# Query projection of a second attention layer by seven block products in place of eight

## The chip, the cores and the metric

The kernel runs on one core of a Trainium2 chip. The metric is the device time of one execution in microseconds. Engines are named as in the profile: PE is TensorE's matmuls and PEld its weight loads, DVE is VectorE, ACT ScalarE, POOL GpSimd, SP the engine that issues most DMAs.

## The reference, cut to what matters

Two gated layers act on x of 16 x 64 tokens by 512, each a cross-attention with 32 query heads and 8 key and value heads of 128 and then a small network. The change is in the attention of the second layer:

```python
q = (hidden_states @ Wq.T).reshape(bsz, q_len, H, HD).transpose(0, 2, 1, 3)
q = _rmsnorm(q, q_norm_w)
k = _rmsnorm(k, k_norm_w)
scores = einsum('bhqd,bhkd->bhqk', q, k) * scale + mask
out = einsum('bhqk,bhkd->bhqd', softmax(scores), v)
return out.reshape(...) @ Wo.T
```

Everything is float32. The kernel splits both operands of each large product into a high and a low part (hi + lo) and sums three matmuls, hi by hi, hi by lo and lo by hi.

## The kernel before

**Tiling.** The 1024 tokens are held transposed, hT_hi and hT_lo of [128, 4, 1024]: four k-tiles of the 512 features on the partitions, tokens along the row. Heads go in 8 groups (g) of J = 4 heads that share a key head, and tokens in two halves (h) of 512. A step (g, h) is one group and one half, unit u = 2g + h. The steps are software-pipelined over three units: step (g, h) projects the queries of unit u, does scores and softmax of unit u - 1 and finishes unit u - 2 with values and the output product. `att_steps` (L881) writes out groups 0, 1 and 7 and loops over 2 to 6.

**TensorE** (`att_pe`, L924 to L1060) does in each steady step of the second layer, in this order: scores of u - 1 (L978), sums of squares for the norm (L953), values of u - 2 (L1005), four heads of projection (`project`, 12 matmuls of 512 columns each through `three`, L226 to L228, into the two banks ps_q) and four token tiles of output product (`project_out`, 12 matmuls each). A head's projection waits for ScalarE's reading (q_rot) of the bank two heads before.

**ScalarE** (`att_act`) computes Ln and Exp of the norm's sums (L1160, L1162), then per head a square (q_sq, L1150) and a copy scaled by the product of the two norm weights (qT, L1153), the high parts of values' results (o_hi, L1191), the softmax exponential (p_sb, L1177), the high part of the probabilities (p_hi, L1184), and the high parts of the next group's weights: wo_hi (L1142) in h = 0, wq_hi (L737) in h = 1.

**VectorE** (`att_dve`, step L1532) does in one step: two transposes of the sums of squares to r_t and eight small copies to r_s (L1457), the transpose of the scores to s_sb (L1435), the scaling by the norm (L1479), the mask (L791), maxima (mx_a L1490, four mx_c L1485), o_lo twice (L1518), two folds of q_sq (L1470), o_lo twice, the sums (sm_a L1502, four sm_c L1485, p_rec), two additions to x_sb (L1529), the transpose of the probabilities (pT, L1512), two folds, p_lo (L808), two additions.

**GpSimd** (`att_pool`, step L1319) does in h = 0 four wo_lo (L1310; the second waits for VectorE's r_s), in h = 1 four wq_lo (L743) between the rest, and in every step the shift of the scores by the maxima (L797) and the normalisation of the probabilities (L803).

**Order and queues.** Each engine works through its list strictly; the order is written by hand in the four `step` functions. SP loads wo, the spilled keys and values and the next wq (`att_wq_split`, L746, waits until both parts of the group before are split). PSUM is full: two banks ps_q, two of ps_s for scores, four ps_b.

## Time and profile before

| | us |
|---|---|
| median of 3 runs | 1179.61 (1178.96 to 1181.38) |
| profiled execution, its own time | 1179.01 |
| span of the profiled execution | 1177.1 |
| a step of the second layer, start of scores to start of scores | 26.08 |

The profile page is one execution. Busy time of PE comes from modelled ends, since matmuls overlap: their pitch is read from the start times in the order of time. TensorE's granted clock is at full speed (2.4 GHz) in all forty slices. In the second layer the scores of step (1,1) start at 787.9, of (2,0) at 813.9, of (2,1) at 840.0, of (3,0) at 866.1, and each next step 26.07 later up to (7,0) at 1074.7.

### The profile page before, as it was taken

Reading aid. Unit: us, or ns where it says so; the run is one execution under the profiler, and the core shown is the slowest. Engines: PE = TensorE matmul, PEld = TensorE weight load, DVE = VectorE, ACT = ScalarE, POOL = GpSimd, SP = SyncE. Lnnn points to the kernel's source line nnn. Section 1 sums busy time; section 2 is a strip of 40 time slices with the busy share of each in tenths; the row PEclk is TensorE's granted clock in tenths of the full one; section 3 lists DMA queues with packets and bytes.
Section 4 is the critical chain, followed back from the end, with each engine's and each line's share of the span. In section 5 each row is a group of like instructions: output and inputs, shape, how many; then the busy total and the mean of one; then the engine's idle time right before and its main releaser. Section 6 shows DMA issues by size and latency. Waiting matters only on the chain.

```text
span 1177.1 us, 17132 instructions
## 1 busy us (share of the span) xinstructions
PE 1169.5 (99%) x6272; PEld 946.7 (80%) x6272; DVE 880.9 (75%) x1538; ACT 424.0 (36%) x748; POOL 532.9 (45%) x371
## 2 busy tenths in 40 slices
PE   9999999999999999999999999999999999999998
PEld 8888888888788888777788888777777777777776
DVE  4656646898888888889984335798888887888695
ACT  5145152322322222231552123535453443435542
POOL 5522533766667676677463112305242433425410
PEclk9999999999999999999999999999999999999999
DMA  7944735812211221211210003121221221121101
GB/s 286 285 137 159 211 111 162 287 55 81 81 66 59 89 80 45 80 45 45 99 64 36 1 1 107 55 94 57 91 80 45 80 80 54 71 89 39 43 1 72
DMA packets 57315, 106.54 MB, mean 91 GB/s; under 512 B 3633, under 2 KB 36529, under 8 KB 51889
## 3 DMA queue, kind: packets, MB, share of 16 engines
q1 hardware_dynamic: 56736, 104.82, 26.0%
q0 software_dynamic: 384, 1.05, 0.2%
q8 instruction: 32, 0.52, 0.2%
q14 instruction: 19, 0.15, 0.0%
q10 hardware_dynamic: 144, 0.00, 0.0%
HBM read 78.59 MB, written 27.26 MB: 90 GB/s over the span
## 4 chain that ended last, share of the span: by engine, by line
PE 96%; DVE 2%; issue 0%; ACT 0%; DVEq 0%; POOL 0%; POOLq 0%
PE ps_q L226 14%; PE ps_b L226 14%; PE ps_b L228 14%; PE ps_b L227 14%; PE ps_q L227 13%; PE ps_q L228 13%; PE ps_s L978 5%; PE ps_b L1005 4%; PE ps_s L278 1%; PE ps_q L953 1%; PE ps_q L2152 1%; PE ps_b L479 1%; PE ps_s L1847 1%; PE ps_q L529 0%; PE ps_b L529 0%
## 5 line engine op out<-in xcount | busy, mean ns | idle before, releaser
L226 PE MATMUL ps_q<-hT_hi,wq_hi 128*128 128x512 f32 x512 | 203.2, 397 | 0.0
L227 PE MATMUL ps_q<-hT_lo,wq_hi 128*128 128x512 f32 x512 | 199.6, 390 | 0.0
L228 PE MATMUL ps_q<-hT_hi,wq_lo 128*128 128x512 f32 x512 | 199.2, 389 | 0.0
L226 PE MATMUL ps_b<-wo_hi,o_hi 128*128 128x512 f32 x440 | 171.6, 390 | 0.0
L227 PE MATMUL ps_b<-wo_lo,o_hi 128*128 128x512 f32 x440 | 171.2, 389 | 0.0
L228 PE MATMUL ps_b<-wo_hi,o_lo 128*128 128x512 f32 x440 | 171.2, 389 | 0.0
L743 POOL TENSOR_TENSOR wq_lo<-wq_raw,wq_hi 128x512 fp32r<-128x512 f32 x64 | 90.2, 1413 | 112.8 <-ACT wq_hi L737 112.8
L1317 POOL TENSOR_TENSOR qT<-q_t 128x512 f32<-128x512 f32 x64 | 89.8, 1405 | 66.3 <-DVE q_t L1430 60.8
L226 PEld LDWEIGHTS ps_q<-hT_hi,wq_hi 128*128 128x128 f32 x512 | 96.1, 188 | 24.3 <-issue 1.5
L228 PEld LDWEIGHTS ps_q<-hT_hi,wq_lo 128*128 128x128 f32 x512 | 96.1, 188 | 20.3
L227 PEld LDWEIGHTS ps_q<-hT_lo,wq_hi 128*128 128x128 f32 x512 | 96.2, 188 | 18.7
L1310 POOL TENSOR_TENSOR wo_lo<-wo_raw,wo_hi 128x512 fp32r<-128x512 f32 x56 | 83.5, 1507 | 56.4 <-ACT wo_hi L1142 38.3
L1184 ACT ACTIVATE p_hi<-pT 128x1024 fp32r<-128x1024 f32 x32 | 34.0, 1061 | 189.7 <-DVE pT L1512 189.7
L226 PEld LDWEIGHTS ps_b<-wo_hi,o_hi 128*128 128x128 f32 x440 | 82.6, 188 | 18.4 <-issue 1.4
L228 PEld LDWEIGHTS ps_b<-wo_hi,o_lo 128*128 128x128 f32 x440 | 82.6, 188 | 17.1
L227 PEld LDWEIGHTS ps_b<-wo_lo,o_hi 128*128 128x128 f32 x440 | 82.6, 188 | 17.1
L1529 DVE SCALAR_TENSOR_TENSOR x_sb<-ps_b,gates,x_sb 128x512 f32<-128x512 f32 x115 | 81.4, 722 | 18.0 <-PE ps_b L228 17.5
L803 POOL TENSOR_TENSOR p_sb<-p_sb,p_rec 128x1024 f32<-128x1024 f32 x29 | 55.7, 1920 | 83.8 <-DVE p_rec L1506 83.8
L1518 DVE TENSOR_TENSOR o_lo<-ps_b,o_hi 128x512 fp32r<-128x512 f32 x128 | 81.8, 682 | 12.6 <-ACT o_hi L1191 10.7
L1191 ACT ACTIVATE o_hi<-ps_b 128x512 fp32r<-128x512 f32 x128 | 66.5, 607 | 34.0 <-PE ps_b L1005 26.7
L1177 ACT ACTIVATE p_sb<-s_sb,zero_b 128x1024 f32<-128x1024 f32 x32 | 37.2, 1162 | 96.9 <-POOL s_sb L797 93.5
L797 POOL TENSOR_TENSOR s_sb<-s_sb,mx_c 128x1024 f32<-128x1024 f32 x28 | 53.8, 1921 | 32.1 <-DVE mx_c L1485 32.1
(301 smaller groups left out, 2498.0 us busy)
## 6 DMA issues: line engine op xcount, KB each, us to landing
wq_raw<-in_wq SPq DMA_DIRECT2D x16, 1024.0 KB, 4.8
wo_raw<-in_wo SPq DMA_DIRECT2D x16, 1024.0 KB, 4.8
kT<-kT_spill SPq DMA_DIRECT2D x32, 256.0 KB, 4.3
v_hi<-v_hi_spill SPq DMA_DIRECT2D x16, 512.0 KB, 3.7
v_lo<-v_lo_spill SPq DMA_DIRECT2D x16, 512.0 KB, 4.7
v_hi_spill<-vs_hi SPq DMA_DIRECT2D x12, 512.0 KB, 5.4
v_lo_spill<-vs_lo SPq DMA_DIRECT2D x12, 512.0 KB, 6.7
kw_raw<-in_wk SPq DMA_DIRECT2D x4, 1024.0 KB, 9.2
```

Source lines behind the costliest of these rows:

```text
L226: nc.tensor.matmul(dst, l_hi, r_hi, start=first, stop=False)
L227: nc.tensor.matmul(dst, l_hi, r_lo, start=False, stop=False)
L228: return nc.tensor.matmul(dst, l_lo, r_hi, start=False, stop=last)
L743: nc.gpsimd.tensor_tensor(wq_lo[:, :, j * D:(j + 1) * D], wq_raw[:, :, j * D:(j + 1) * D], wq_hi[:, :, j * D:(j + 1) * D].bitcast(F32), AL ...
L797: eng.tensor_tensor(sc, sc, wide(mx_c[:, :], QB), ALU.subtract).then_inc(c["s_shifted"], 1)
L803: eng.tensor_tensor(pr, pr, wide(p_rec[:, :], QB), ALU.mult).then_inc(c["p_normed"], 1)
L978: last = nc.tensor.matmul(ps_s[par * S:(par + 1) * S, t * JS:(t + 1) * JS], kT[:, h, b:b + S], qT[:, h, :, b:b + S], start=True, stop=True)
L1191: nc.scalar.activation(o_hi[:, 2 * half:2 * half + 2, :, par * S:(par + 1) * S], ps_b[n].rearrange("p (t j q) -> p t j q", t=2, j=J), ACT. ...
L1310: nc.gpsimd.tensor_tensor(lo, wo_raw[:, j, :], hi.bitcast(F32), ALU.subtract).then_inc(c["wo_lo"], 1)
L1317: nc.gpsimd.tensor_tensor(qT[:, h, j, :], q_t1[:, j % 2, :], q_t2[:, j % 2, :], ALU.add).then_inc(c["q_rot"], 1)
L1518: nc.vector.tensor_tensor(o_lo[part], ps_b[n].rearrange("p (t j q) -> p t j q", t=2, j=J), o_hi[part].bitcast(F32), ALU.subtract).then_inc ...
L1529: nc.vector.scalar_tensor_tensor(x_sb[:, i, :], out_bank(u, t)[:, :], gates[:, lay:lay + 1], x_sb[:, i, :], ALU.mult, ALU.add).then_inc(c[ ...
```

## The change

For groups W0 = 3 to 6 of the second layer (`woven`), the product of the 512 x 512 weights of a group and the 512 x 512 tokens of a half is cut into 2 x 2 blocks of 256 and computed by seven block products and sums of blocks:

- of the weights (blocks a11, a12, a22 and one below s1's place): s1, s2, s3, s4, four sums of [128, 2, 256] on GpSimd in float32 (`woven_sums` in h = 0 of the group before, `woven_last_sum` in h = 1), and seven high parts on ScalarE and seven low parts on GpSimd in place of four of each; all 512 elements a partition;
- of the tokens: t1 to t4, [128, 2, 512] each for both halves, once, on GpSimd in steps (1,0) to (2,1), 10 operations of 1024 elements; four high parts on ScalarE, four low parts on GpSimd;
- each product is 12 matmuls of 256 columns (two head columns, two k-tiles, three parts), 84 in a step where there were 48 of 512;
- of the results: two products accumulate in one bank (a11 with a12, s3 with a22, s1 with s4); ScalarE copies the first product to qT, and VectorE makes five joins of a PSUM bank with a part of qT (512 elements each). The first head pair's first block is copied by ScalarE alone.

In these steps ScalarE also makes the eight r_s copies (the function `last_sums`, L1164, that was used once, renamed), VectorE folds the squares in two operations of [64, 4, 256] in place of four of [64, 2, 256], the transposed probabilities are written to s_sb and not to pT (so the scores' transpose waits for p_lo), and VectorE adds one output tile before and three after the turn of the probabilities in place of two and two. Steps (2,0), (2,1), (6,0) and (6,1) are written out, not in the loop. The norm weights are multiplied into the keys in the first phase (ScalarE, `kv_stage_keys`) and their DMA and product move there; the query copies lose their scale. Some semaphore increments that nobody waits for go, and buffers move. One launch argument, the scratch size for dynamic DMAs, becomes 2048.

The diff, cut to its core:

```diff
+        WOVEN_PARTS = ("a11", "s2", "s3", "a12", "s1", "a22", "s4")
+        def woven_sums(pool, gt):
...
+            nc.gpsimd.tensor_tensor(s1_f, s1_f, a22, ALU.add).then_inc(c["s_f"], 1)
+            nc.gpsimd.tensor_tensor(s2_f[:, :, :], s1_f, a11, ALU.subtract).then_inc(c["s_f"], 1)
+            nc.gpsimd.tensor_tensor(s3_f[:, :, :], a22, s2_f[:, :, :], ALU.subtract).then_inc(c["s_f"], 1)
+            def project_woven(g, h):
...
+                def product(bank, name, right, first, last_one=False):
+                    if h == 0:
+                        pe.wait_ge(*c("woven_hi", turn)); pe.wait_ge(*c("woven_lo", turn))
+                    for q in range(2):
+                        for k in range(2):
...
+                pe.wait_ge(*c("ssq_t", u))
+                if h == 0:
+                    pe.wait_ge(*c("t_hi", 4))
+                    pe.wait_ge(*c("t_lo", 4))
+                product(ps_q[0], "a11", tokens(0, 0), True).then_inc(c["product"], 1)
+                product(ps_q[1], "s2", mixed(t2_hi, t2_lo), True, True).then_inc(c["product"], 1)
+                pe.wait_ge(*c("s_turned", u))
+                product(ps_h[0], "s3", mixed(t3_hi, t3_lo), True).then_inc(c["product"], 1)
+                pe.wait_ge(*c("copied", n + 1))
+                product(ps_q[0], "a12", tokens(1, 0), False, True).then_inc(c["q_done"], 1)
+                product(ps_h[1], "s1", mixed(t1_hi, t1_lo), True).then_inc(c["q_done"], 1)
+                pe.wait_ge(*c("joined", 5 * n + 2))
+                product(ps_h[0], "a22", mixed(t4_hi, t4_lo), False, True).then_inc(c["q_done"], 1)
+                pe.wait_ge(*c("joined", 5 * n + 3))
+                product(ps_h[1], "s4", tokens(1, 1), False, True).then_inc(c["q_done"], 1)
@@ ScalarE
+            def woven_step(g, h, next_wq):
+                sums_by_quadrant(us)
+                norms(us)
+                nc.scalar.activation(qT[:, h, 0:2, late], heads(ps_q[0]), ACT.Copy).then_inc(c["copied"], 1)
+                for n in range(4): out_high(up, n)
+                nc.scalar.activation(q_sq[:, 0:2, early], heads(ps_q[0]), ACT.Square).then_inc(c["q_sq"], 1)
+                nc.scalar.activation(qT[:, h, 0:2, early], heads(ps_q[0]), ACT.Copy).then_inc(c["q_rot"], J)
+                exponentials(us)
...
+                probs_high(us)
@@ GpSimd
+            def woven_step(g, h, next_wq):
+                if h == 0:
+                    for name in WOVEN_PARTS[4:]:
+                        woven_low(pool, g, name)
+                    for j in range(J):
+                        wo_low(g - 1, j)
+                elif building:
+                    woven_low(pool, g + 1, "a11")
+                att_shift(pool, lay, u - 1)
+                if h and building:
+                    woven_last_sum(pool, g + 1)
+                att_normalise(pool, lay, u - 1)
+                if h == 0 and not (isinstance(g, int) and g == G - 2):
+                    woven_sums(pool, g + 1)
+                elif building:
+                    for name in WOVEN_PARTS[1:4]:
+                        woven_low(pool, g + 1, name)
+                if second_opening(lay, g, h):
+                    att_normalise(pool, lay, us)
+                    pool.wait_ge(*c("p_lo", us + 1))
+                    mixed_first(t1_f, t1_t, (0, 1), (0, 0))
+                    mixed_joined(t1_f, t1_t, 3)
+                if (g, h) == (1, 1):
+                    att_wq_low(pool, lay, 2, 0)
+                    att_shift(pool, lay, us)
+                    pool.wait_ge(*c("p_exp", us + 1))
+                    mixed_first(t3_f, t3_t, (1, 1), (0, 1))
+                    att_normalise(pool, lay, us)
+                    for j in range(1, J):
+                        att_wq_low(pool, lay, 2, j)
+                    pool.wait_ge(*c("p_lo", us + 1))
+                    mixed_joined(t3_f, t3_t, 6)
+                    mixed_next(t2_f, (1, 1), t1_f, 8, 3)
+                if (g, h) == (2, 0):
+                    for j in range(J):
+                        wo_low(1, j)
+                    att_shift(pool, lay, us)
+                    pool.wait_ge(*c("p_exp", us + 1))
+                    mixed_next(t4_f, (1, 0), t2_f, 10, 8)
+                    att_normalise(pool, lay, us)
+                    woven_sums(pool, W0)
+                    pool.wait_ge(*c("p_lo", us + 1))
+                    mixed_low(t1_lo, t1_hi, t1_f, 1)
+                if builds_woven(lay, g, next_wq):
+                    mixed_low(t3_lo, t3_hi, t3_f, 2)
+                    woven_last_sum(pool, W0)
+                    att_shift(pool, lay, us)
+                    pool.wait_ge(*c("p_exp", us + 1))
+                    mixed_low(t2_lo, t2_hi, t2_f, 3)
+                    woven_low(pool, W0, "a11")
+                    att_normalise(pool, lay, us)
+                    for name in WOVEN_PARTS[1:4]:
+                        woven_low(pool, W0, name)
+                    mixed_low(t4_lo, t4_hi, t4_f, 4)
@@ VectorE
+            def woven_step(g, h):
+                turn_sums(us, 1 - h, True)
+                turn_scores(us, 1 - h)
+                scale_scores(us)
+                joined(part_b, ps_q[1], part_b)
+                att_mask(dve, lay, us, 1 - h)
+                joined(part_d, ps_h[0], part_b)
+                maxima(us)
+                joined(part_d, ps_h[1], part_d)
+                out_low(up, 0)
+                out_low(up, 1)
+                joined(qT[:, h, 2:4, early], ps_h[0], part_b)
+                out_low(up, 2)
+                joined(part_b, ps_h[1], part_b)
+                out_low(up, 3)
+                sums(us)
+                add_output(up, h, 0)
+                fold_woven(u, 0)
+                turn_probs(us)
+                fold_woven(u, 1)
+                att_probs_low(dve, lay, us)
+                for t in range(1, PAIRS):
+                    add_output(up, h, t)
```

## Rows read from the trace of the kernel before

**Rows 1.** Page: engines' busy us, share, instructions; the ending chain by engine

```profile
PE 1169.5 (99%) x6272; PEld 946.7 (80%) x6272; DVE 880.9 (75%) x1538; ACT 424.0 (36%) x748; POOL 532.9 (45%) x371
...
PE 96%; DVE 2%; issue 0%; ACT 0%; DVEq 0%; POOL 0%; POOLq 0%
```

**Rows 2.** Order of time, TensorE: start us, us, line, tiles; one step, the next's start

```profile
918.23 1.95 PE L978 MATMUL ps_s<-qT,kT 128*64 128x256 f32 x16
...
920.70 0.39 PE L1005 MATMUL ps_b<-p_hi,v_hi 64*128 64x256 f32 x2
920.93 0.28 PE L1005 MATMUL ps_b<-p_lo,v_hi 64*128 64x256 f32 x2
...
922.12 0.28 PE L1005 MATMUL ps_b<-p_hi,v_lo 64*128 64x256 f32 x2
922.32 0.50 PE L226 MATMUL ps_q<-hT_hi,wq_hi 128*128 128x512 f32 x1
...
944.31 1.95 PE L978 MATMUL ps_s<-qT,kT 128*64 128x256 f32 x16
```

**Rows 3.** Order of time, TensorE, opening of the layer; and one group of the whole span

```profile
741.20 0.39 PE L228 MATMUL ps_q<-hT_hi,wq_lo 128*128 128x512 f32 x1
741.43 0.60 PE L278 MATMUL ps_s<-ident,ln_buf 128*128 128x128 f32 x4
...
L278 PE MATMUL ps_s<-ident,ln_buf 128*128 128x128 f32 x92 | 12.4, 273 | 0.4 <-DVE ln_buf L266 0.2 <-DVE hT_lo L288 0.2
```

**Rows 4.** Order of time, VectorE: the last addition of that step

```profile
944.42 0.75 DVE L1529 SCALAR_TENSOR_TENSOR x_sb<-ps_b,gates,x_sb 128x512 f32<-128x512 f32 x1 [0.18 <-PE ps_b L228]
```

**Rows 5.** Order of time of the same step: GpSimd, then VectorE

```profile
923.38 5.83 POOL L1310 TENSOR_TENSOR wo_lo<-wo_raw,wo_hi 128x512 fp32r<-128x512 f32 x3 [3.05 <-DVE r_s L1457]
...
923.25 1.25 DVE L1435 STREAM_TRANSPOSE s_sb<-ps_s 128x1024 f32<-128x1024 f32 x1
924.61 1.23 DVE L1479 TENSOR_TENSOR s_sb<-s_sb,r_q 128x1024 f32<-128x1024 f32 x1
925.87 2.20 DVE L791 TENSOR_TENSOR s_sb<-s_sb,mask_sb 128x1024 f32<-128x1024 f32 x1
928.10 1.22 DVE L1490 TENSOR_REDUCE mx_a<-s_sb 128x32 f32<-128x1024 f32 x1
```

**Rows 6.** Groups, 866 to 1075: xcount, busy us, mean ns; last: one line's min/median/max ns

```profile
L1529 DVE SCALAR_TENSOR_TENSOR x_sb<-ps_b,gates,x_sb 128x512 f32<-128x512 f32 x34 | 24.7, 726 | 11.0 <-PE ps_b L228 11.0
...
L1518 DVE TENSOR_TENSOR o_lo<-ps_b,o_hi 128x512 fp32r<-128x512 f32 x32 | 20.6, 686 | 6.1 <-ACT o_hi L1191 4.9
...
L743 POOL TENSOR_TENSOR wq_lo<-wq_raw,wq_hi 128x512 fp32r<-128x512 f32 x16 | 20.8, 1298 | 64.8 <-ACT wq_hi L737 64.8
...
L797 POOL TENSOR_TENSOR s_sb<-s_sb,mx_c 128x1024 f32<-128x1024 f32 x8 | 15.4, 1921 | 6.8 <-DVE mx_c L1485 6.8
...
L1457 DVE COPY r_s<-r_t 32x16 f32<-32x16 f32 x64 | 10.7, 167 | 1.4
...
L1485 DVE TENSOR_TENSOR mx_c<-mx_a 32x32 f32<-32x32 f32 x32 | 5.9, 186 | 0.6
...
L791 DVE TENSOR_TENSOR s_sb<-s_sb,mask_sb x15: 1217/1226/2203, 752.4 to 1126.1; 128x1024 f32<-128x1024 f32 x15
```

**Rows 7.** GpSimd's durations of L808; order of time: VectorE in (1,0), TensorE in (3,0)

```profile
L808 POOL TENSOR_TENSOR p_lo<-pT,p_hi x13: 2382/2397/3464, 243.2 to 550.6; 128x1024 fp32r<-128x1024 f32 x13
...
786.92 0.69 DVE L1470 TENSOR_TENSOR q_sq<-q_sq 64x512 f32<-64x512 f32 x1
787.64 1.23 DVE L808 TENSOR_TENSOR p_lo<-pT,p_hi 128x1024 fp32r<-128x1024 f32 x1
...
870.18 0.50 PE L226 MATMUL ps_q<-hT_hi,wq_hi 128*128 128x512 f32 x1
```

**Rows 8.** ScalarE's durations (min/median/max ns) of two lines

```profile
L1171 ACT ACTIVATE r_s<-r_t x8: 226/228/230, 1121.2 to 1122.9; 32x16 f32<-32x16 f32 x8
...
L1160 ACT ACTIVATE r_q<-r_s,eps_rms x16: 321/322/323, 749.7 to 1123.1; 128x32 f32<-128x32 f32 x16
```

More of the change, by code:

```diff
@@ L945, in project @@
                 last.then_inc(c["q_done"], 1)
+            def project_woven(g, h):
+                u = 2 * g + h
+                n = u - 2 * W0
+                left = {name: woven_parts(name)[1:] for name in WOVEN_PARTS}
+                tok = [slice(h * HALF + a * QT, h * HALF + (a + 1) * QT) for a in range(2)]
+                own = slice(h * QT, (h + 1) * QT)
+                tokens = lambda rows, a: (hT_hi[:, 2 * rows:2 * rows + 2, tok[a]], hT_lo[:, 2 * rows:2 * rows + 2, tok[a]])
+                mixed = lambda hi, lo: (hi[:, :, own], lo[:, :, own])
+                def product(bank, name, right, first, last_one=False):
+                    if h == 0:
+                        turn = 7 * (g - W0) + WOVEN_PARTS.index(name) + 1
+                        pe.wait_ge(*c("woven_hi", turn))
+                        pe.wait_ge(*c("woven_lo", turn))
+                    l_hi, l_lo = left[name]
+                    r_hi, r_lo = right
+                    for q in range(2):
+                        for k in range(2):
+                            col = slice(q * D, (q + 1) * D)
+                            dst, closes = bank[:, q * QT:(q + 1) * QT], last_one and (q, k) == (1, 1)
+                            nc.tensor.matmul(dst, l_hi[:, k, col], r_hi[:, k, :], start=first and (q, k) == (0, 0), stop=False, skip_group_check=True)
+                            nc.tensor.matmul(dst, l_hi[:, k, col], r_lo[:, k, :], start=False, stop=False, skip_group_check=True)
+                            last = nc.tensor.matmul(dst, l_lo[:, k, col], r_hi[:, k, :], start=False, stop=closes, skip_group_check=True)
+                    return last
+                pe.wait_ge(*c("ssq_t", u))
[13 more added lines that the diff above has]
+                product(ps_h[1], "s4", tokens(1, 1), False, True).then_inc(c["q_done"], 1)
@@ L1067, in step @@
                         values(up, h, g - 1)
+                if woven(lay, g):
+                    project_woven(g, h)
+                    for t in range(PAIRS):
+                        project_out(up, h, g - 1, t)
+                    return
                 at_first = lay and isinstance(g, int) and (g, h) == (0, 0)
@@ L1152, in queries @@
                     ln_high(act, lns[2], NT - 1)
[L1153 removed]
+                nc.scalar.activation(qT[:, h, j, :], bank[:, :], ACT.Copy).then_inc(c["q_rot"], 1)
             def norms(u):
@@ L1434, in turn_scores @@
                 dve.wait_ge(*c("scored", u + 1))
+                if lay and not (isinstance(u, int) and (u < 4 or u == 2 * G - 1)):
+                    dve.wait_ge(*c("p_lo", u))
                 nc.vector.transpose(s_sb[:, :], ps_s[:, :]).then_inc(c["s_turned"], 1)
@@ L1471, in fold_squares, with fold_woven @@
                     dve.wait_ge(*c("q_fold", 4 * u + 2 * pair + r + 1))
+            def fold_woven(u, r):
+                own, tok = fold_part(r)
+                other = fold_part(1 - r)[0]
+                dve.wait_ge(*c("q_sq", 4 * u + 2 * r + 2))
+                nc.vector.tensor_tensor(q_sq[own, :, tok], q_sq[own, :, tok], q_sq[other, :, tok], ALU.add).then_inc(c["q_fold"], 2)
             def scale_scores(u):
@@ L1534, in step @@
                 if before_closing(lay, g, h):
+                    return
+                if woven(lay, g):
+                    woven_step(g, h)
                     return
```

278 lines of the change are left out of this document (239 added, 39 removed).

## The prediction

> **What bounds the kernel now.** I read the page's engine line and chain line first. TensorE shows work in 1169.5 of 1177.1 us, VectorE in 880.9, GpSimd in 532.9, ScalarE in 424.0. The chain of waits that ends last is TensorE for 96% and VectorE for 2% [rows 1]. So the end is set by the number of matmuls and their pitch, and by any moment at which TensorE must wait. The profiled execution took 1179.01 us (span 1177.1 and 1.9 around it), 0.6 under the median 1179.61 of the runs; I sum against the execution and give the result against the median.
>
> TensorE's own order of time shows one step of the second layer [rows 2]: scores at 918.23, values at 920.70, query projection at 922.32, and the next step's scores at 944.31. A step is 26.08 us, and no row in it shows a wait. I write times as distance from the step's start: values at 2.47, the projection at 4.09. A 512-column matmul comes every 0.227 us (0.23 by the rounded starts [rows 3]), so 48 of the projection take 10.9 and 48 of the output product another 10.9.
>
> VectorE has 1.6 us of slack at the end of a step: its last x_sb addition ends at 945.17, and the values that need its bank come at 944.31 + 2.47 = 946.78 [rows 2, 4]. Beside it, the two orders of time of VectorE and GpSimd for the same microseconds matter most [rows 5]. The mask addition takes 2.20 us where a run without GpSimd beside it takes 1.22, and three wo_lo subtractions take 5.83 together where three of their size, as wq_lo at 1.30, would take 3.9 [rows 5, 6]. The score scaling at 924.61 was not slowed, the mask after it was: a GpSimd operation that stood queued ran between the two, then the mask, then the next. So a VectorE operation with both inputs in SBUF and a GpSimd operation run one after the other. Reductions, transposes and operations that read PSUM (o_lo 0.69, x_sb 0.73 [rows 6]) run undisturbed beside GpSimd: mx_a at 928.10 takes its usual 1.22.
>
> The Trainium skill, SBUF — State Buffer, says the same where it lists which operations take the port that the two engines share: an exclusive lock for the whole instruction, taken by a VectorE instruction with two SBUF inputs against a GpSimd one that reads SBUF. By that rule all of GpSimd's new subtractions contend, and the trace agrees (2.20 against 1.22).
>
> **The change, part by part.** *TensorE.* In eight steps (groups 3 to 6, two each) 48 matmuls of 512 columns become 7 x 12 = 84 of 256 columns, each with its own full weight load. No row has this shape. Pairs of 256-column matmuls on half the rows come every 0.119 us (ten pitches from 920.93 to 922.12) [rows 2], and 128-column matmuls with a full weight load each every 0.11 (four in 0.60, of which the record of one is 0.27) [rows 3], so the load can keep up with 0.11. I take 0.120, the nearest row in columns: 84 x 0.120 = 10.1, minus 10.9, is -0.8 a step, -6.4 in all. The bounds are 0.11 (-1.6 a step, -13) and 0.130, where the gain is nil.
>
> The Trainium skill, TensorE: Matmul & The Clock Gate, section on packing small matmuls, says that a weight load overlaps matmuls in flight only when its row group differs. By that, load and stream add up for each of the 84. The sum does not use it: at 0.227 for 512 columns in the same row groups the trace disagrees.
>
> *VectorE, steady.* Added per step are five joins (PSUM plus qT, 512 elements): 5 x 0.69 = 3.5 (as o_lo [rows 6]). Eight r_s copies of 0.167 go to ScalarE (-1.4), four folds of 0.69 [rows 7] become two of 1.22, my estimate from the mask's 1024 elements (-0.3). Net +1.8 in a step with 1.6 of slack. The copies on ScalarE take 8 x 0.24 = 1.9 and Ln and Exp 0.32 each [rows 8]. r_t is ready when today's copies begin, 1.4 before the transpose at 5.02 [rows 5], so r_q comes at 3.6 + 1.9 + 0.7 = 6.2, no later than today's scaling at 6.38. ScalarE, 36% busy, has room for the rest: its qT copies lose a scale, it squares and copies as much as before.
>
> *The place where it bites.* The last product needs the third join, which the diff puts behind scale, join, mask, join and the maxima. Products start at 4.1 + n x 1.44: the seventh could start at 12.7. VectorE, second half of a group: scale 6.4 to 7.6, join 8.3, mask 9.5, join 10.2, mx_a 11.4, four mx_c of 0.186 12.2, join 12.9: 0.2 late. First half of a group: GpSimd now has seven queued subtractions there (three woven weights, four wo_lo) in place of four, so the mask waits 1.0 as today: 13.9, 1.2 late. That is 1.4 for two steps. If a mx_c also meets a subtraction it is one more microsecond, if none does nothing; both kept.
>
> *End of a step.* The first fold stands before the turn of the probabilities and has two SBUF inputs, so it waits for GpSimd's normalisation (1.92), then takes 1.22, where today the turn follows at once. p_lo and three additions then end near 28 to 30, against values at 26.1 + 2.5 = 28.6 [rows 2]. I take 0.35 a step. So the steady stretch is 4 x 1.4 + 8 x 0.35 = +8.4 against -6.4: +2.0.
>
> *GpSimd before group 3.* Ten operations on 128x1024 build the four token mixes, four more take their low parts. With two full SBUF inputs 1024 elements take 2.40 [rows 7], so 14 x 2.4 = 33.6 us, none of which exists today. All must be done between p_lo of step (1,0), which ends at 788.87, and the projection of (3,0) at 870.18 [rows 7]: 81.3 us. In the same window GpSimd has four wq_lo and four wo_lo (8 x 1.3), six shifts and normalisations (6 x 1.92 [rows 6]) and eight woven sums and splits (8 x 1.3): 32.3. Total 65.9. VectorE's operations that exclude GpSimd count per step (eight r_s 1.34, scale 1.23, mask 1.22, mx_c and sm_c 8 x 0.186, folds 4 x 0.69, p_lo 1.23), 9.3 in all and 27.8 in three steps [rows 5 to 7]. The two together need 93.7 in 81.3. A queued subtraction holds the port for less than its record: wo_lo, mask and wo_lo follow each other from 925.84 to 929.21, which leaves 1.08 for each wo_lo [rows 5]. Since not all will queue I take 0.12 off each of 36, 4.3. So the window must grow by 8.1 even with no gap. I take 8.1. Late r_s and mx_c are what TensorE will feel: r_q comes late, ScalarE's query copies stand behind it in its queue, and the third head's projection waits for them; in (2,0) the output product waits for wo_lo, queued behind 7.2 us of mixes. The bounds: 0 if the port yields more than I read, and 18 with the gaps: GpSimd waits for the exponential (1.2) in three steps and both engines for each other's softmax part, about 2 a step.
>
> *The rest.* The norm weights' product and their DMA move into the first phase: the DMA is issued before x's, for which VectorE waits in the same place, and the scale goes from ScalarE's query copies to its key copies, an engine in use 36% of the time. Nothing. The DMA of the query weights waits for all seven splits; these end in the next step, its data is needed a step later. Nothing, unless GpSimd runs over a whole step.
>
> **Sum.** -6.4 + 8.4 + 8.1 = +10.1, or 1179.0 + 10.1 = 1189.1 for the profiled execution and **1189.7** for the median.
>
> **Rivals.** *The port does not decide (faster).* If GpSimd's operations fall into VectorE's reductions, transposes and PSUM reads, only the products' 6.4 remains: 1173.2. For it: these free stretches make up over half of VectorE's step, and two waits in the diff (for p_exp, for p_lo) keep mixes out of part of the exclusive work. Against it: 93.6 in 81.3, and the mask is delayed today with four subtractions queued. It decides where fewer than one exclusive operation per step is held up.
>
> *The port decides more (slower).* Every one of eight small copies or four mx_c can meet another queued 2.4 us mix; the bound 18 in place of 8.1, so 1199.6.
>
> *The products are not cheaper.* At a pitch of 0.14 the 84 take 11.8, +0.9 a step; the joins then wait less, and +7 replaces about +2: 1194.7. Serial loading is a rival of its own: 0.120 + 0.109 = 0.229 each, 19.2 for 10.9, +66: about 1255. The 512-column pitch speaks against it; it is the skill's packing rule named above.
>
> *A draw.* If the transition costs 4 in place of 8.1 and no product waits in first halves, the sum is near 0: 1179.6.
>
> **How the numbers follow.** My forecast has 0.44 (its own range 1184 to 1196), the faster rival 0.24, the draw 0.10, the worse port 0.16, the dear products 0.05, serial loading 0.01. About 0.2% is what a measurement of this kernel can tell from no change. Faster is 0.24, same 0.10, slower 0.44 + 0.16 + 0.05 + 0.01 = 0.66. The range for 8 in 10 is 1173 to 1203: below it the cheap pitches of the faster rival, above it the worst of the port and serial loading.
>
> **What would show it.** Right: the 256-column rows at 0.12 pitch; steps of groups 3 to 6 near 26.3 on average, with TensorE idle before the seventh product released by VectorE's qT; mask, r_s, mx_c and folds with means far above their clean ones; the start of group 3's scores at 874, not 866. Wrong: steps of 25.3, or scores of group 3 at 866, or r_s copies at 0.167 all through.

## The result, and the profile after

The changed kernel takes 1202.08 us (median of 6, 1201.29 to 1203.65), the kernel before, run beside it, 1179.45 (6 runs, 1178.96 to 1181.38). The ratio is 1.0191, 95% interval 1.0178 to 1.0204: 22.6 us slower, where 10.1 had been forecast; it lies 0.9 below the upper end of the range. The profiled execution took 1201.29, with a span of 1199.5 against 1177.1, so 22.4 us have to be found.

Below, the *mixes* are GpSimd's fourteen operations for t1 to t4 (ten for the blocks, four low parts), a *pair* is the steps (g,1) and (g+1,0), and an instruction is *held* when it lasts longer than the same instruction does with the other engine idle.

The page of the changed kernel, engines and the ending chain by engine, answers to [rows 1]:

```profile
PE 1170.2 (98%) x6560; PEld 956.9 (80%) x6560; DVE 931.7 (78%) x1498; ACT 438.0 (37%) x812; POOL 624.4 (52%) x413
...
PE 73%; DVE 20%; issue 6%; ACT 1%; POOL 1%; DMA 0%; DVEq 0%; SPq 0%; ACTq 0%
```

TensorE has as many busy us as before in a longer span. VectorE's share of the chain went from 2% to 20%, and 6% is "issue". GpSimd got 91.5 us more, VectorE 50.8, though VectorE has 40 instructions fewer.

Where the time went is read from the starts of the scores of each step. The stretches between them, in the windows view of the changed kernel (columns: stretch, length, busy us and instructions of PE, PEld, DVE, ACT, POOL, granted TensorE clock, DMA share, GB/s):

```profile
787.60:819.60 32.00, 26.83 (x154) 20.77 (x155) 30.28 (x39) 13.80 (x25) 21.40 (x11) 1.00 0.12 42
819.60:854.00 34.40, 30.45 (x154) 23.34 (x154) 31.12 (x39) 10.69 (x18) 24.48 (x14) 0.85 0.20 69
854.00:883.80 29.80, 26.56 (x153) 20.52 (x152) 28.24 (x39) 15.60 (x28) 19.32 (x12) 1.00 0.13 45
883.80:911.60 27.80, 26.85 (x188) 22.05 (x188) 25.70 (x33) 10.00 (x22) 22.21 (x13) 0.94 0.24 86
911.60:937.20 25.60, 25.21 (x189) 21.61 (x188) 23.51 (x34) 13.53 (x29) 14.32 (x8) 1.00 0.15 52
937.20:964.60 27.40, 25.52 (x191) 21.70 (x190) 25.46 (x34) 12.19 (x26) 21.08 (x13) 1.00 0.25 86
...
1095.40:1124.10 28.70, 27.14 (x163) 20.86 (x162) 23.65 (x38) 13.21 (x24) 17.73 (x11) 1.00 0.13 47
```

The scores of (1,1) start at 787.57, in the kernel before at 787.71 (not at 787.9, as stated above for it): what moved into the first phase costs nothing. Steps (1,1), (2,0) and (2,1) took 96.3 us; the kernel before has 78.4 there (26.23, 26.07, 26.07). That is 17.9 of the 22.4. I call these three steps the opening. Step (3,0), the first of the new kind, is 1.7 longer than before; the seven after it lose 1.2 together (a pair is 52.9 against 52.14); (7,0), a plain step behind them, takes 28.7 in place of 27.1, 1.6 more.

The opening, in the order of time of the changed kernel (start us, us, engine, line, operation), GpSimd's and VectorE's rows of one stretch together, then TensorE's:

```profile
788.81 2.38 POOL L1558 TENSOR_TENSOR t_f<-hT_hi 128x1024 f32<-128x1024 f32 x1 [4.06 <-DVE p_lo L918]
791.15 2.39 POOL L1559 TENSOR_TENSOR t_t<-hT_lo 128x1024 f32<-128x1024 f32 x1
793.62 2.40 POOL L1563 TENSOR_TENSOR t_f<-t_f,t_t 128x1024 f32<-128x1024 f32 x1
...
791.04 5.74 DVE L1785 COPY r_s<-r_t 32x16 f32<-32x16 f32 x8
...
809.43 2.93 DVE L1820 TENSOR_TENSOR sm_c<-sm_a 32x32 f32<-32x32 f32 x4
...
816.06 3.41 DVE L1798 TENSOR_TENSOR q_sq<-q_sq 64x512 f32<-64x512 f32 x2
...
824.66 8.47 DVE L1785 COPY r_s<-r_t 32x16 f32<-32x16 f32 x8
...
819.56 3.51 PE L1136 MATMUL ps_s<-qT,kT 128*64 128x256 f32 x16 [3.24 <-issue]
...
830.62 0.39 PE L255 MATMUL ps_q<-hT_hi,wq_lo 128*128 128x512 f32 x1
834.96 0.76 PE L253 MATMUL ps_q<-hT_hi,wq_hi 128*128 128x512 f32 x1 [3.95 <-ACT qT L1316]
835.52 0.63 PE L254 MATMUL ps_q<-hT_lo,wq_hi 128*128 128x512 f32 x1
...
883.83 2.94 PE L1136 MATMUL ps_s<-qT,kT 128*64 128x256 f32 x16 [2.32 <-DVE q_sq L1798]
```

Eight copies of 0.167 us each [rows 6] take 5.74 in (1,1) and 8.47 in (2,0): a copy ends only when the GpSimd operation beside it ends, GpSimd then starts the next one, and a copy behind waits again. Eleven of the 24 copies of the opening were held, for up to 2.3 us; four of those in (2,0) by a wo_lo of 1.3 and not by a mix. The query norm's factors come late by that much, ScalarE's query copies stand behind them, and TensorE waits 3.95 for the bank.

The waits of 3.24 and 2.32 are of another kind: scores need the folded squares, and the folds stand beside low parts on GpSimd; before the 3.24, beside wq_lo, they take 3.41 for two of 0.69 (they end at 819.47, the scores start at 819.56).

Behind the 3.95 twelve matmuls come every 0.425 and not every 0.227; the sixteen scores behind the 3.24 take 3.51 and not 1.95. The granted clock of 834.9 to 840.2 is 0.50 and of 819.5 to 823.1 it is 0.54, that is the lower of TensorE's two levels, 1.2 GHz. The two cost 2.4 + 1.6 = 4.0 us on top of the waits. Behind the 2.32 the clock of 884.4 to 887.8 is 0.53: 3.4 us at the lower level, by my estimate 1.7 lost, in (3,0).

GpSimd itself is not the limit of the opening: the windows above have it busy 21.4 + 24.5 + 19.3 = 65.2 us of 96.2, idle for 31. Nor do the shift and the normalisation stand behind mixes: from (1,1) to (7,0) each of them starts 0.08 us after VectorE's instruction that releases it.

Groups of the changed kernel, 780 to 1100 us (xcount, busy us, mean ns, idle before and its releaser), which answer to [rows 6]:

```profile
L1806 DVE TENSOR_TENSOR q_sq<-q_sq 64x1024 f32<-64x1024 f32 x16 | 34.0, 2122 | 0.5
...
L918 DVE TENSOR_TENSOR p_lo<-s_sb,p_hi 128x1024 fp32r<-128x1024 f32 x10 | 22.1, 2206 | 0.3
L1875 DVE TENSOR_TENSOR qT<-ps_s,qT 128x512 f32<-128x512 f32 x32 | 21.8, 682 | 0.3
...
L1785 DVE COPY r_s<-r_t 32x16 f32<-32x16 f32 x24 | 18.9, 786 | 0.4
...
L1163 PE MATMUL ps_b<-p_hi,v_hi 64*128 64x256 f32 x92 | 14.6, 305 | 8.5 <-DVE x_sb L1864 8.4
```

The 24 copies of the three opening steps took 18.9 where they would be 4.0. The joins cost what was said (0.682, read from PSUM, undisturbed), but the new folds take 2.12 and not 1.22. TensorE's idle time in the woven steps (groups 3 to 6) stands before the values and is ended by VectorE's last x_sb; before the seventh product it is 1.6 in all. The end of (4,1) and the values of (5,0) behind it, in the order of time, with a row of the end of (4,0) last, answer to [rows 2, 4, 5]:

```profile
997.37 0.28 PE L1085 MATMUL ps_q<-t_lo,s_hi 128*128 128x256 f32 x1
997.49 0.28 PE L1086 MATMUL ps_q<-t_hi,s_lo 128*128 128x256 f32 x1
...
994.09 0.39 PE L1163 MATMUL ps_b<-p_hi,v_hi 64*128 64x256 f32 x2 [1.41 <-DVE x_sb L1864]
...
983.32 1.92 POOL L913 TENSOR_TENSOR p_sb<-p_sb,p_rec 128x1024 f32<-128x1024 f32 x1 [2.62 <-DVE p_rec L1841]
985.20 3.55 POOL L825 TENSOR_TENSOR s_lo<-s_f,s_hi 128x512 fp32r<-128x512 f32 x2
...
983.85 2.48 DVE L1806 TENSOR_TENSOR q_sq<-q_sq 64x1024 f32<-64x1024 f32 x1
...
987.51 2.32 DVE L1806 TENSOR_TENSOR q_sq<-q_sq 64x1024 f32<-64x1024 f32 x1
989.86 2.20 DVE L918 TENSOR_TENSOR p_lo<-s_sb,p_hi 128x1024 fp32r<-128x1024 f32 x1
...
963.24 2.20 DVE L918 TENSOR_TENSOR p_lo<-s_sb,p_hi 128x1024 fp32r<-128x1024 f32 x1
```

The new products come every 0.12. At the end of (4,1) the first fold stands behind the normalisation (2.48 for 1.22), the second fold (2.32) and p_lo (2.20) behind low parts of the next weights, and the values of (5,0) come 1.41 late. At the end of (4,0) only the first fold and p_lo (the row at 963.24, behind a sum of weights) are held, and the values of (4,1) come 0.38 late.

### The profile page after: what moved, and what is told of

It reads as the page before. It is cut to its first block, busy times and chain, and to the rows that moved or that the text cites. A ratio compares the mean times of both kernels' runs of the same rounds, so it can differ in the third digit from the quotient of the medians.

```text
span 1199.5 us, 17752 instructions
## 1 busy us (share of the span) xinstructions
PE 1170.2 (98%) x6560; PEld 956.9 (80%) x6560; DVE 931.7 (78%) x1498; ACT 438.0 (37%) x812; POOL 624.4 (52%) x413
## 4 chain that ended last, share of the span: by engine, by line
PE 73%; DVE 20%; issue 6%; ACT 1%; POOL 1%; DMA 0%; DVEq 0%; SPq 0%; ACTq 0%
PE ps_b L253 10%; PE ps_b L255 10%; PE ps_b L254 10%; PE ps_q L253 10%; PE ps_q L255 9%; PE ps_q L254 9%; PE ps_s L1136 3%; PE ps_b L1163 3%; DVE o_lo L1853 2%; DVE x_sb L1864 2%; DVE qT L1875 2%; DVE q_sq L1806 2%; DVE r_s L1785 2%; DVE mx_a L1825 1%; DVE sm_a L1837 1%
## 5 line engine op out<-in xcount | busy, mean ns | idle before, releaser
L253 PE MATMUL ps_q<-hT_hi,wq_hi 128*128 128x512 f32 x384 | 154.0, 401 | 4.9 <-ACT qT L1316 4.9
L254 PE MATMUL ps_q<-hT_lo,wq_hi 128*128 128x512 f32 x384 | 150.7, 392 | 0.0
L255 PE MATMUL ps_q<-hT_hi,wq_lo 128*128 128x512 f32 x384 | 150.4, 392 | 0.0
L253 PEld LDWEIGHTS ps_b<-wo_hi,o_hi 128*128 128x128 f32 x440 | 82.6, 188 | 19.5 <-issue 2.8
L253 PEld LDWEIGHTS ps_q<-hT_hi,wq_hi 128*128 128x128 f32 x384 | 72.7, 189 | 25.0 <-issue 5.9
L255 PEld LDWEIGHTS ps_q<-hT_hi,wq_lo 128*128 128x128 f32 x384 | 72.6, 189 | 15.6
L254 PEld LDWEIGHTS ps_q<-hT_lo,wq_hi 128*128 128x128 f32 x384 | 72.7, 189 | 14.1
L849 POOL TENSOR_TENSOR wq_lo<-wq_raw,wq_hi 128x512 fp32r<-128x512 f32 x48 | 71.8, 1506 | 23.0 <-ACT wq_hi L769 23.0
L1354 ACT ACTIVATE o_hi<-ps_b 128x512 fp32r<-128x512 f32 x128 | 66.9, 608 | 34.9 <-PE ps_b L1163 27.6
L675 POOL TENSOR_TENSOR kw_lo<-kw_raw,kw_hi 128x512 fp32r<-128x512 f32 x28 | 36.2, 1297 | 68.9 <-ACT kw_hi L631 68.9
```

Source lines behind the costliest of these rows:

```text
L253: nc.tensor.matmul(dst, l_hi, r_hi, start=first, stop=False)
L254: nc.tensor.matmul(dst, l_hi, r_lo, start=False, stop=False)
L255: return nc.tensor.matmul(dst, l_lo, r_hi, start=False, stop=last)
L849: nc.gpsimd.tensor_tensor(wq_lo[:, :, j * D:(j + 1) * D], wq_raw[:, :, j * D:(j + 1) * D], wq_hi[:, :, j * D:(j + 1) * D].bitcast(F32), AL ...
L1354: nc.scalar.activation(o_hi[:, 2 * half:2 * half + 2, :, par * S:(par + 1) * S], ps_b[n].rearrange("p (t j q) -> p t j q", t=2, j=J), ACT. ...
```

## The experiments

My theory after the result: each instruction of VectorE that excludes GpSimd waits for one whole queued operation, small or large, and what costs is how many of them meet one (the port). Its rivals: GpSimd's queue is simply longer, so that its shift, normalisation and wo_lo come late (the queue); and VectorE is full with five more joins (the joins). All differences are against the kernel before, run on the same chip.

**e1, without the token mixes.**

```diff
-                nc.gpsimd.tensor_tensor(by_half(f), quarters(hT_hi, *l), quarters(hT_hi, *r), ALU.subtract).then_inc(c["t_f"], 1)
+                return
...
-                mixed = lambda hi, lo: (hi[:, :, own], lo[:, :, own])
+                mixed = lambda hi, lo: tokens(0, 1)
```

> The changed kernel without the four token mixes: their ten operations, four high and four low parts are left out, and the products that use them read plain tokens. If GpSimd's token mixes are what the transition costs (17.7 of the 22.6 us at the start of group 3's scores), the scores of (2,0), (2,1) and (3,0) start within 1 us of the kernel before, and only the rest, 22.6 - 17.7 = 4.9, stays: about 1184.5. If the copies' and weights' work of the woven steps, or the longer first woven step, are behind it, the scores of group 3 still start more than 10 us late and the time stays above 1195.

1183.27, +3.8. The steps to (2,0) are back at 26.07 to 26.23, (2,1) takes 26.96 and (3,0) 26.23; group 3's scores start 0.9 later than their distance before. So the mixes, with their high and low parts, are 17.0 of the opening's 17.9, and most of (3,0)'s loss.

**e2, the mixes as memsets.**

```diff
-                nc.gpsimd.tensor_tensor(f[:, :, :], f[:, :, :], t[:, :, :], ALU.add).then_inc(c["t_f"], 1)
+                for n in range(3):
+                    last = nc.gpsimd.memset(t[:, :, :].bitcast(F32), 0.0)
```

> The changed kernel in which each of the fourteen GpSimd operations of the token mixes is replaced by three memsets of the same buffer, each behind the one before, about 2.4 to 2.7 us together: GpSimd is as long busy in the same places of its queue and the same engines wait for it, but it reads no SBUF there. If the port shared by VectorE and GpSimd makes the loss, VectorE's r_s and sm_c copies go back to 0.17 to 0.19 us and most of the 17.7 us before group 3 goes: 3 to 6 stay for GpSimd's longer queue, 1186 to 1191 in all. If GpSimd's queue alone makes it (shift, normalisation and wo_lo standing behind the mixes), the time stays near 1202. If a write alone holds the port too, the copies stay long and the time near 1202.

1203.59, +24.1: no better. The order of time of e2 shows why:

```profile
789.37 2.97 POOL L1560 MEMSET t_f<- 128x1024 f32 x3 [4.04 <-DVE p_lo L918]
...
791.61 6.92 DVE L1797 COPY r_s<-r_t 32x16 f32<-32x16 f32 x8
...
808.68 2.98 POOL L1560 MEMSET t_f<- 128x1024 f32 x3 [1.25 <-ACT p_sb L1340]
...
811.18 0.77 DVE L1832 TENSOR_TENSOR sm_c<-sm_a 32x32 f32<-32x32 f32 x4
```

The third case of the expectation came, so e2 did not part port from queue. In e2 the queue does delay something: a stand-in takes 3.0 us and a mix 2.4, and the normalisation starts 2.2 and 2.3 us after it could in (1,1) and (2,0).

**e3, ScalarE makes r_s in the opening too.**

```diff
-                if by_scalar or isinstance(u, int) and u == 2 * G - 1:
+                if by_scalar or isinstance(u, int) and (u == 2 * G - 1 or 2 <= u <= 4):
...
+                    if isinstance(us, int) and 2 <= us <= 4:
+                        sums_by_quadrant(us)
                     norms(us)
```

> The changed kernel in which ScalarE makes the eight r_s copies in steps (1,1), (2,0) and (2,1) too, as it does in groups 3 to 6; all mixes stay. By the port theory each of VectorE's small copies waits for a whole 2.4 us operation that is queued on GpSimd: in the trace 14 of the copies took 1.31 us on average and not 0.17, most of them here. Then 7 to 10 of the 17.7 us go: 1192 to 1195. By the queue theory VectorE's copies don't matter: 1201 to 1203.

1194.59, +15.1: 7.5 us less than the changed kernel, for 24 copies of 0.167. The opening costs 9.2 in place of 17.9, inside the range that the port theory gave; of the 8.7 won there (3,0), 28.6 long, loses 0.8 again. Its trace also says what the 9.2 are: the shift and the normalisation start 0.08 us after their release in every step, so GpSimd's queue delays neither, and VectorE's two-input instructions are held:

```profile
794.43 3.41 DVE L1816 TENSOR_TENSOR s_sb<-s_sb,r_q 128x1024 f32<-128x1024 f32 x1 [1.56 <-ACT r_q L1325]
797.87 2.20 DVE L901 TENSOR_TENSOR s_sb<-s_sb,mask_sb 128x1024 f32<-128x1024 f32 x1
...
807.88 2.93 DVE L1822 TENSOR_TENSOR sm_c<-sm_a 32x32 f32<-32x32 f32 x4
```

**e9, the opposite: VectorE makes r_s in the woven steps too.**

```diff
-                turn_sums(us, 1 - h, True)
+                turn_sums(us, 1 - h)
...
-                sums_by_quadrant(us)
                 norms(us)
```

> The changed kernel with one part of the change undone: in the woven steps VectorE makes the eight r_s copies again, not ScalarE. Clean they are 1.34 us of VectorE's time a step, and ScalarE's chain to r_q gets 0.6 shorter. By the port theory the copies of the second step of each pair, where GpSimd has seven operations of 1.3 us queued, each meet one: several us of VectorE's time a pair, 1206 to 1214. If the port did not matter for so short an instruction, 1200 to 1204.

1221.57, +42.4, 19.5 above the changed kernel and beyond what was expected. Its order of time in (4,0):

```profile
947.62 6.34 DVE L1784 COPY r_s<-r_t 32x16 f32<-32x16 f32 x8
...
948.40 4.99 POOL L1542 TENSOR_TENSOR wo_lo<-wo_raw,wo_hi 128x512 fp32r<-128x512 f32 x4
...
955.48 0.54 PE L1084 MATMUL ps_s<-t_hi,s_hi 128*128 128x256 f32 x1 [3.88 <-DVE s_sb L1762]
```

The copies cost 5.0 more than clean; the transpose of the scores comes behind them, the third product needs its bank and waits 3.88, and the matmuls behind are slow again (granted clock 0.50 from 955.5 to 958.9). A pair takes 57.7. The part of the change that gives these copies to ScalarE is what makes the rest bearable.

**e13, memsets and ScalarE's r_s together.**

```diff
+                for n in range(3):
+                    last = nc.gpsimd.memset(t[:, :, :].bitcast(F32), 0.0)
...
+                if by_scalar or isinstance(u, int) and (u == 2 * G - 1 or 2 <= u <= 4):
```

> e2 (memsets in the place of the token mixes, 1203.6) and e3 (ScalarE's r_s copies in the opening steps, 1194.6) together. In e2's trace the r_s copies alternate with the memsets (6.9 us for eight, 1.34 clean), but four sm_c additions ran beside a memset in 0.77 us where beside a mix they took 2.9, and a p_lo in 1.22. If the exclusion is one between an instruction of VectorE with two inputs in SBUF and one of GpSimd that reads SBUF, and r_s is the only kind that a pure write holds up, no VectorE instruction meets a mix any more: 1186 to 1190, only GpSimd's queue (3.0 us for each mix, longer than before) being left. If the queue carries a large part of the loss, 1194 or more, no better than e3.

1192.73, +13.6, between the two ranges. No VectorE instruction is held by a stand-in any more (scale and mask 1.23 and 1.22 beside memsets in (1,1)), though folds and mx_c still are by wq_lo, wo_lo, the shift and weights' sums (3.97 for two folds in (2,0)), and GpSimd's own order then sets the pace:

```profile
834.06 6.02 POOL L1562 MEMSET t_f<- 128x1024 f32 x6 [1.24 <-ACT p_sb L1340]
840.04 1.92 POOL L913 TENSOR_TENSOR p_sb<-p_sb,p_rec 128x1024 f32<-128x1024 f32 x1
...
836.65 0.35 DVE L1855 RECIPROCAL p_rec<-sm_c 128x32 f32<-128x32 f32 x1
```

The normalisation could start at 837.0 and starts at 840.04, behind the t4 operations; VectorE's turn of the probabilities waits 3.76 for it, and TensorE 5.07 at the next scores. So a queue long enough costs time by itself. But each stand-in is 3.0 here, and with mixes of 2.4 in the changed kernel and in e3 the same normalisation starts 0.08 after its release: this cost is of e13 and e2 alone.

**e4, another order of the weights' work in the woven steps.**

```diff
-                att_normalise(pool, lay, u - 1)
                 if h == 0 and not (isinstance(g, int) and g == G - 2):
                     woven_sums(pool, g + 1)
                 elif building:
-                    for name in WOVEN_PARTS[1:4]:
-                        woven_low(pool, g + 1, name)
-                elif next_wq:
+                    woven_low(pool, g + 1, "s2")
+                att_normalise(pool, lay, u - 1)
+                if building:
+                    woven_low(pool, g + 1, "s3")
+                    pool.wait_ge(*c("p_lo", u))
+                    woven_low(pool, g + 1, "a12")
+                elif h and next_wq:
```

> The changed kernel with another order of GpSimd's queue in the woven steps alone: the three sums of weights before the normalisation of the probabilities and not behind it, one low part before it, and the last low part of the next weights and all behind it held until VectorE's p_lo is done. The same operations, the same joins on VectorE. If the port makes the steady loss (p_lo at 2.2 and the fold at 2.5 for 1.22 clean, TensorE 1.4 late with the values of each second step), that idle time goes and a pair of steps takes 51.5 in place of 52.9: some 4 us in three and a half pairs, 1198. If VectorE's five joins make it, the pair stays at 52.9 and the time near 1202.

1198.49, +19.0: 3.6 less for the same operations. A pair takes 51.96, p_lo is clean,

```profile
963.89 1.23 DVE L918 TENSOR_TENSOR p_lo<-s_sb,p_hi 128x1024 fp32r<-128x1024 f32 x1
```

and the idle time before the values is gone from (4,0), (5,0) and (6,0); (3,0) still has 1.90 and (7,0) 1.56. In its place the seventh product waits 0.99 for the third join in (4,0) and (5,0) and 0.53 in (6,0).

**e6 and e7, GpSimd's or VectorE's new work left out.** e6 leaves the weights' sums and their parts out of e1, e7 the joins:

```diff
 e6
-            nc.gpsimd.tensor_tensor(s1_f, s1_f, a22, ALU.add).then_inc(c["s_f"], 1)
+            return
 e7
-                    return nc.vector.tensor_tensor(out, heads(bank), part, ALU.add)
+                joined = lambda out, bank, part: left_out
```

> e1 (no token mixes, 1183.3, a pair of woven steps 52.9), and in the woven steps GpSimd's four sums of weights and the high and low parts of s2, s3 and s4 are left out too; the products that use them read token blocks as weights. GpSimd then has no more to do than in the kernel before, VectorE keeps its five joins. If the GpSimd work makes the steady loss, a pair takes under 51.4 and the whole 1177 to 1179. If the joins make it, a pair stays above 52.4 and the whole at 1182 to 1184.

> e1 (no token mixes, 1183.3, a pair of woven steps 52.9) with VectorE's five joins of each woven step left out (3.5 us of its time a step) and the waits for them; GpSimd keeps all weights' work. If the joins make the steady loss a pair takes 50.6 to 51.4 and the whole 1176 to 1179. If GpSimd's queue makes it, 52 and more, 1181 to 1183. If each is enough alone, since VectorE has only 1.6 us of slack, both e6 and e7 gain.

1178.43 and 1177.51, -0.7 and -1.6 (ratios 0.9993, 0.9984 to 1.0002, and 0.9985, 0.9975 to 0.9994). A pair is 51.9 and 51.2, where e1 has 52.9 and the kernel before 52.14. The windows of one pair of e7:

```profile
944.90:970.20 25.30, 25.30 (x191) 21.73 (x190) 20.93 (x29) 13.40 (x29) 13.82 (x9) 1.00 0.15 52
970.20:996.10 25.90, 25.34 (x191) 21.70 (x190) 23.12 (x30) 12.09 (x26) 20.97 (x12) 1.00 0.26 91
```

e6's pair lies between its two ranges, e7's inside that of the joins. Both gain, as the third case says for two loads on one slack. TensorE's own time is 25.13 to 25.3 a step, so seven products in place of eight do give 0.8 to 0.9 a step.

**e10, no mixes and the better order; e12, the third join earlier on top.**

```diff
 e12
-                maxima(us)
+                part_maxima(us)
+                if h:
+                    whole_maxima(us)
                 joined(part_d, ps_h[1], part_d)
+                if h == 0:
+                    whole_maxima(us)
```

> e1 (no token mixes, 1183.3) with the order of weights of e4 and the held low parts of (6,1): what the seven products would give if the token mixes were free. e4 took 1.0 us off each pair and 1.1 more off the last one: 1183.3 - 3.5 - 1.5 for the last x_sb of (6,1) = 1178.3, within 1.5. If it is above 1180.5, the steady steps can't be better than before by order alone.

> e10 (no token mixes, 1179.1) with the third join moved in the same way. Its trace has three waits of 1.0 us for that join. If they go without another in their place, 1176.1; if VectorE is full, 1179 as before. Beside e11 it tells what the token mixes still cost once they are placed well.

e10 1179.10, ratio 1.0000 (0.9991 to 1.0009), as expected; e12 1181.12, 1.0016 (1.0007 to 1.0025), above both its cases. Windows of a pair of e12:

```profile
946.50:972.40 25.90, 25.41 (x191) 21.73 (x190) 23.75 (x35) 13.52 (x29) 11.01 (x7) 1.00 0.15 51
972.40:999.00 26.60, 25.94 (x189) 21.86 (x188) 23.72 (x33) 11.96 (x26) 19.54 (x13) 1.00 0.25 89
```

The waits for the join are gone, but TensorE waits 0.59 for o_lo in (4,0) and 0.49 before the values of (4,1), and the second halves of the groups, 25.28 in e10, take 25.85. VectorE is the second bound: what it does sooner for one product is late for the next. And even with free mixes the change is a draw.

**e5, e8, e11, the mixes placed elsewhere.** Each has e3's and e4's edits. e5 spreads the fourteen operations over (0,1) to (2,1); e8 is e5 with GpSimd's queue held in five places; e11 is e8 and moves the third join as e12 does, and s4's sum behind the shift.

```diff
 e8, against e5, one of the five places
                     mixed_joined(t1_f, t1_t, 6)
-                    att_wq_low(pool, lay, 2, 1)
-                    att_wq_low(pool, lay, 2, 2)
+                    pool.wait_ge(*c("p_lo", us + 1))
+                    for j in range(1, J):
+                        att_wq_low(pool, lay, 2, j)
                     mixed_high_side(t2_f, (1, 1), t1_f, 6)
-                    att_wq_low(pool, lay, 2, 3)
```

> All operations of the changed kernel, with the scalar sums of e3 and the order of weights of e4, and the fourteen operations of the token mixes spread over steps (0,1) to (2,1), singly or in pairs, most of them placed where VectorE does transposes, reductions and reads of PSUM. GpSimd has the same amount to do. If what counts is how many of VectorE's operations meet a queued one, 2 to 4 us of the 17.9 stay: 1181 to 1185. If GpSimd simply has too much to do before group 3 (65.9 us of its own in 81.3, and VectorE's exclusive ones besides), it can't come below 1190.

> e5 (1185.6) with GpSimd's queue held until VectorE's p_lo is done in four more places: before the last three wq_lo of (1,1), before the weights' sums of (2,0), and before the last low parts of (2,1) and of (6,1); and until the first two folds are done before the low part of t4. In e5's trace these are where a fold took 1.6 to 2.8 for 0.69 and p_lo 3.3 and 2.2 for 1.22, and TensorE stood 2.1, 1.9 and 0.8 us. No operation is added or left out. By the port theory 4 to 6 us go: 1179.5 to 1182. If the held operations then come too late for TensorE themselves, 1185 and more.

> e8 (1184.4) with two moves: in the second step of each pair VectorE makes the third join right behind mx_a and before the four mx_c copies, and in (2,1) GpSimd's sum for s4 stands behind the shift. In e8's trace the seventh product of (3,0) waits 3.5 us for the third join, since three mx_c copies each met a wo_lo, and the matmuls behind it run at half pitch; in each later pair it waits 1.0. If the late third join is what is left, (3,0) gets 4 to 5 us shorter and each pair 1.0: 1176.5 to 1179. If VectorE as a whole is full and the loss only moves to its last additions to x_sb, 1182 and more.

e5 1185.61 (+6.5), e8 1184.38 (+5.3), e11 1184.80 (+5.6). Step (1,1)'s end in e5, where a mix stands queued,

```profile
814.37 3.29 DVE L918 TENSOR_TENSOR p_lo<-pT,p_hi 128x1024 fp32r<-128x1024 f32 x1
...
813.76 2.82 POOL L1579 TENSOR_TENSOR t_f<-hT_hi,t_f 128x1024 f32<-128x1024 f32 x1
```

and in e8, where it is held; behind it the first woven step of e8:

```profile
812.22 1.23 DVE L918 TENSOR_TENSOR p_lo<-pT,p_hi 128x1024 fp32r<-128x1024 f32 x1
...
880.37 3.32 DVE L1845 TENSOR_TENSOR mx_c<-mx_a 32x32 f32<-32x32 f32 x4
...
884.65 0.35 PE L1084 MATMUL ps_s<-hT_hi,s_hi 128*128 128x256 f32 x1 [3.54 <-DVE qT L1900]
...
885.41 0.42 PE L1086 MATMUL ps_s<-hT_hi,s_lo 128*128 128x256 f32 x1
```

In e8 steps (1,1) and (2,0) take 26.2 and 26.1, as before, and the whole opening loses 1.6 and not 17.9. But (3,0) now takes 30.8: three mx_c copies meet a wo_lo, the third join is 3.5 late, and the matmuls behind it run at half pitch. In e11 that wait is gone, but the scores of (3,0) wait 2.23 for the folds, o_lo comes 1.59 late, (3,0) takes 28.8 and (2,1) 28.6, and 5.6 us stay. e5 ended 0.6 above the range of the count and far below the 1190 that too large a load on GpSimd would need; e8 between its two cases; e11 in the second, VectorE full. A GpSimd operation that is made to wait is owed later.

**The opening over all runs.** The time for which VectorE's instructions were held in the three opening steps (duration minus clean duration, 0.17, 0.19, 0.69 and 1.22 us, summed from the orders of time; an estimate) and what the opening lost:

| run | held, us | opening longer by, us |
|---|---|---|
| before | 2.8 | 0 |
| e6 | 5.1 | 0.0 |
| e1 | 8.6 | 0.9 |
| e8 | 9.7 | 1.6 |
| e11 | 10.7 | 2.5 |
| e5 | 15.1 | 4.6 |
| e3 | 22.8 | 9.2 |
| changed kernel | 30.6 | 17.9 |

e7, e10 and e12 are within 0.1 of e1 in both columns; e4 and e9, with the changed kernel's opening, have 30.1 and 30.0 for 17.9 and 17.8. The two go together wherever the shift and the normalisation follow their release at once. In e13 (12.3 and 9.3) and e2 (26.0 and 20.2), where stand-ins delay them, the loss is larger than the row of that size.

## Why the prediction was right or wrong

- **Right: TensorE.** Pitch 0.120 forecast, 0.119 measured; a step without a wait takes 25.1 for 26.07. Serial loading (1255) and a pitch of 0.14 did not come. The gain of 6.4 was there (0.94 in (6,1), which has no wait; 0.8 a step in e6 and e10).
- **Wrong: the size of the transition, "I take 8.1".** It measured 17.9, and (3,0) another 1.7. The step that failed is the sum "93.7 in 81.3". Its GpSimd part was right (65.9 forecast, 65.2 busy), but it adds the loads of two engines as if each wait were made up by work of the other, and takes VectorE's exclusive instructions at their clean 27.8. They were held for 30.6 on top (table above), while GpSimd was idle for 31 of 96.2 us: while the copies stand at 824.66 to 833.1 in front of the transpose, the scaling and the mask, GpSimd comes to the end of its queue, and then stands idle for 6.22 us before the shift at 839.14, whose maxima are late. The costs come in sequence on one chain. e5 shows it from the other side: the same operations, placed elsewhere, cost the opening 4.6.
- **A rival near by number.** *The port decides more* gave 1199.6, and the upper bound of 18 was the size. Its reason (small copies that each meet a mix) is partly right: eleven of 24 copies were held, four of them by wo_lo and not by a mix, and the scores waited for folds, which it does not name; 4.0 us of clock were not in it. That its sum comes so near is in part luck. A chance of 0.16 was too small.
- **Missed in that term: the clock.** After TensorE's waits of 3.24 and 3.95 us it ran at the lower level, 4.0 us more, and after 2.32 another 1.7 in (3,0). No row of the kernel before had such a wait.
- **Not the cause: GpSimd's order.** The prediction let the output product of (2,0) wait for wo_lo behind mixes. No such wait came, and shift and normalisation were never late. e13 and e2 show that they can be, with stand-ins of 3.0.
- **Steady steps: +2.0 forecast, 1.7 + 1.2 = 2.9 measured, and the terms are not those forecast.** Waits for the third join: 5.6 forecast in eight steps, 1.6 measured. Ends of steps: 2.8 forecast (0.35 each), 5.9 measured, 1.4 in (4,0) and (5,0), 1.5 in (6,0), 0.4 to 0.5 in the others except (6,1). The clock of (3,0), 1.7, was not forecast. That the total is near is luck. The mis-sized part is the folds (1.22 taken, 2.12 measured) and p_lo (1.22, 2.20). Both terms are VectorE's fullness, as e4, e10 and e12 show: take it from one place and it is at the other.
- **Wrong: "the rest, nothing".** The move into the first phase did cost nothing. But (7,0) loses 1.6, since three wq_lo stand beside the folds and p_lo at the end of (6,1). Held back (e8, e10) (7,0) takes 27.5 to 27.6 and not 28.7; without joins (e7) it takes 27.7, so here too one load less is enough.
- **The faster rival** needed the port not to decide; e3 and e9 exclude that. **The draw** needed an opening of 4. Placed as in e5 and e8 the opening costs 4.6 and 1.6, but with the other terms these versions are 6.5 and 5.3 slower; 1179.1 exists only without the mixes (e10).
- **The signs.** Group 3's scores start at 883.8, not 874. Steps of groups 3 to 6 take 26.4 on average, 26.3 forecast. TensorE's idle time before the seventh product, ended by qT, is there, but small.

No version tried that computes everything beats the kernel before. Open: how much of each held microsecond reaches TensorE. The table above gives pairs of numbers, not a rule.

## What to carry to other kernels

When work goes to GpSimd beside a busy VectorE, don't compare sums of busy time: go through VectorE's exclusive instructions one by one, the smallest first, and charge each that can meet a queued operation up to one whole operation, in sequence on its chain. If the engine with the large new load turns out to be idle part of the time, as GpSimd here, its load is not the limit. Put small copies on ScalarE, and GpSimd's bulk work where VectorE transposes, reduces or reads PSUM, held there by a wait; then look what the held work is late for. A product made cheaper by sums is only worth what the engine that makes the sums has free.

## What had not been expected of the hardware

- A VectorE copy of 32x16 elements, 0.17 us clean, took up to 2.3 us beside queued GpSimd operations, eight in a row taking 5.7 and 8.5; a held copy ends with the operation beside it (in (2,0) five in a row), and one or two copies run between two GpSimd operations.
- A GpSimd memset, which reads nothing, holds such copies up as well (6.92 for eight), but not VectorE instructions with two inputs (in e2 sm_c 0.77 for four and p_lo 1.22, in e13 scale 1.23 and mask 1.22).
- Waits of TensorE of 2.32, 3.24 and 3.95 us (3.54 in e8) were followed by matmuls at half pitch, with a granted clock of 0.50 to 0.64 in the 3 us behind the wait. Behind waits of 0.9 to 1.6 us the pitch stayed as it was. Waits between went both ways: the clock behind 1.92 in e3 was 0.56 and behind 2.23 in e11 0.63, but 1.00 behind 2.23 in e3 and behind 2.26 in e2.
